# Column hats made on ScalarE from one loaded row of columns, in place of twelve hats loaded by DMA; two buffers of them instead of three

## What is computed

```python
x = x + _L0_conv_ref(_gn(x), ...)   # 3x3 convolution in Winograd form (6x6 tiles, weights given in the tile domain)
x = x + _L1_conv_ref(_gn(x), ...)   # offsets by a 3x3 convolution, then a deformable 3x3 convolution, 8 groups
x = x + _L2_conv_ref(_gn(x), ...)   # four 3x3 convolutions with one-bit weights, quantised activations
x = x + _L3_conv_ref(_gn(x), ...)   # 3x3 convolution, vertical edges, channel attention
return x
```

```python
y0 = jnp.floor(py)
x0 = jnp.floor(px)
corners = [(y0, x0, (y0 + 1 - py) * (x0 + 1 - px)), (y0, x0 + 1, (y0 + 1 - py) * (px - x0)),
           (y0 + 1, x0, (py - y0) * (x0 + 1 - px)), (y0 + 1, x0 + 1, (py - y0) * (px - x0))]
```

## Time and profile before

| | |
|---|---|
| median of 3 runs | 4374.5 us (4368.3 to 4380.27) |
| the profiled execution | 4387.05 us, its span 4385.2 us |
| busy, share of the span | TensorE 95%, GpSimd 70%, VectorE 67%, ScalarE 42% |
| granted TensorE clock, mean | 0.983 of full speed |
| DMA | 1022.94 MB, mean 233 GB/s |
| DMA queues, share of 16 engines | q1 474.56 MB, 35.8%; q10 342.81 MB, 23.7%; q0 201.52 MB, 16.1% |

### The profile page before, as it was taken

One profiled execution on the slowest core, in us unless ns is written; L12 is line 12 of the kernel. 1 busy time (PEld: TensorE's weight loads), 2 busy tenths in 40 slices (PEclk: granted clock), 3 DMA queues, 4 the chain that ended last, 5 costly groups with the idle time before them and its releaser, 6 DMA issues.

```text
span 4385.2 us, 67257 instructions
## 1 busy us (share of the span) xinstructions
PE 4187.6 (95%) x24997; PEld 2015.3 (46%) x24997; DVE 2945.6 (67%) x6076; ACT 1831.5 (42%) x2008; POOL 3077.7 (70%) x3094
## 2 busy tenths in 40 slices
PE   2899999999999999999999999999999999999993
PEld 2444444444444544444454444444444454444441
DVE  5656677667766766777677767766776676666553
ACT  1343444444444434444444444444444443444431
POOL 1777777777776767767777776777767677776740
PEclk8999999999999999999999999999999999999996
DMA  4677787878877787887878878787787878778762
GB/s 109 217 245 230 234 263 224 259 229 247 257 239 232 237 248 247 244 251 230 249 240 250 260 233 255 224 259 228 242 258 231 249 237 251 247 243 251 224 194 63
DMA packets 480252, 1022.94 MB, mean 233 GB/s; under 512 B 262164, under 2 KB 298356, under 8 KB 475636
## 3 DMA queue, kind: packets, MB, share of 16 engines
q1 hardware_dynamic: 311668, 474.56, 35.8%
q10 hardware_dynamic: 69984, 342.81, 23.7%
q0 software_dynamic: 98304, 201.52, 16.1%
HBM read 862.19 MB, written 73.20 MB: 213 GB/s over the span
## 4 chain that ended last, share of the span: by engine, by line
PE 81%; POOL 5%; DMA 5%; DVE 5%; issue 2%; SPq 2%; ACTq 1%; ACT 0%; POOLq 0%; DVEq 0%
PE ps_r L1489 58%; PE ps_y L1501 6%; PE ps_c L1475 6%; POOL ring L600 5%; PE ps_a L1428 3%; DMA taps_c<-plane_act 3%; PE ps_c L1515 2%; PE ps_a L1475 1%; PE ps_y L1522 1%; PE ps_a L1466 1%; DMA plane_act<-act_c 1%; PE ps_c L1570 1%; DVE work_c L1271 1%; PE ps_c L1548 1%; ACTq L790 1%
## 5 line engine op out<-in xcount | busy, mean ns | idle before, releaser
L600 POOL DMA_INDIRECT ring<-patch_table,idx_part x3072 | 3069.5, 999 | 1153.9 <-issue 1001.5
L1489 PE MATMUL ps_r<-select,image 128*128 128x512 f32 x6912 | 3151.4, 601 | 14.1 <-DVE col_hat L1195 9.5
L1489 PEld LDWEIGHTS ps_r<-select,image 128*128 128x128 f32 x6912 | 1259.6, 191 | 1401.6 <-issue 1383.6
L1195 DVE TENSOR_TENSOR col_hat<-ps_r,col_hat 128x512 f32<-128x512 f32 x1152 | 793.0, 688 | 1219.4 <-PE ps_r L1489 1215.1
L650 ACT ACTIVATE select<-row_in,minus_row 128x1536 f32<-128x1536 f32 x384 | 604.6, 1575 | 994.4 <-PE ps_r L1489 615.9
L652 ACT ACTIVATE select<-select,one_col 128x1536 f32<-128x1536 f32 x384 | 605.4, 1577 | 12.5
L669 ACT COPY samples<-ps_c 128x512 f32<-128x512 f32 x256 | 148.8, 581 | 638.3 <-PE ps_c L1515 638.1
L1501 PEld LDWEIGHTS ps_y<-col_hat,w_dense 128*32 128x32 f32 x9216 | 228.2, 109 | 291.1 <-issue 289.5
L1501 PE MATMUL ps_y<-col_hat,w_dense 128*32 128x128 f32 x9216 | 331.2, 277 | 0.0
L1204 DVE TENSOR_TENSOR ps_w<-ring,ps_w 128x384 f32<-128x384 f32 x512 | 284.5, 556 | 40.2 <-DMA ring<-patch_table,idx_part 35.9
L1210 DVE TENSOR_TENSOR ring<-ring,ps_w 128x384 f32<-128x384 f32 x512 | 279.9, 547 | 4.4
(11 more groups left out here) (231 smaller groups left out, 2414.6 us busy)
## 6 DMA issues: line engine op xcount, KB each, us to landing
row_in<-coord_table ACTq DMA_DIRECT2D x384, 768.0 KB
col_hat<-coord_table SPq DMA_DIRECT2D x384, 768.0 KB
ring<-patch_table,idx_part POOLq DMA_INDIRECT x3072
taps_c<-plane_act SPq DMA_DIRECT2D x135, 268.1 KB
coord_table<-wino SPq DMA_DIRECT2D x64, 216.0 KB
taps_c<-xn_c ACTq DMA_DIRECT2D x96, 130.0 KB
taps_c<-xn_c SPq DMA_DIRECT2D x96, 130.0 KB
plane_act<-act_c SPq DMA_DIRECT2D x180, 65.0 KB
```

The lines of the kernel that those rows point to most:

```text
L600: nc.gpsimd.indirect_dma_start(out=ring[j][:, h % 2, k, :], out_offset=None, in_=table, in_offset=bass.IndirectOffsetOnAxis(ap=idx_part[:, ...
L1195: v.tensor_tensor(hat_t, ps_r[:, (s + t) % 2], hat_t, ALU.mult).then_inc(tile_weighed, 1)
L1489: ins = mm(ps_r[:, (s + t) % 2], image[:, m, t], select[s % 2][:, m], start=(m == 0), stop=(m == PAIRS - 1))
```

## The change

The coordinates table now holds 7 rows for each part in place of 18: six for the row hats and the column coordinate itself. VectorE writes the column with one copy in place of 12 subtractions, and ScalarE's two activations in slot 21 are gone; SyncE waits for VectorE alone. For each slot SyncE loads 512 columns, broadcast over 128 partitions (256 KB written in place of 768 KB), into one of two `col_in` buffers. ScalarE makes the hats for slot s+1 in slot s (`make_cols`): three Abs activations of 128 x 512, each with its own column number as bias (`minus_col`), and one Relu of 128 x 1536 over all three. It waits for the DMA and for the fold that frees one of now two `col_hat` buffers. VectorE's `weigh_tile` waits for `cols_made` in place of the DMA. `load_cols` waits for `col_in_read`, which ScalarE raises behind `make_cols` two slots earlier, and no longer for `dense_folded`. The biases are made once at the start, by one GpSimd iota and eight small VectorE instructions.

```diff
@@ -56,7 +56,8 @@
 WT = WIN // WQ
-ROWS = 2 * PAIRS + WIN
+ROWS = 2 * PAIRS + 1
 EPS = 1e-5
...
@@ -229,7 +232,8 @@
         select = [sb(f"select{b}", [P, PAIRS, HALF]) for b in range(2)]
-        col_hat = [sb(f"col_hat{b}", [P, WT, HALF]) for b in range(3)]
+        col_in = [sb(f"col_in{b}", [P, HALF]) for b in range(2)]
+        col_hat = [sb(f"col_hat{b}", [P, WT, HALF]) for b in range(2)]
         image = sb("image", [P, PAIRS, WT, P])
...
@@ -453,13 +461,11 @@
                 part = coord_table[bass.ds((n % 2) * ITEMS + (dense_tap(e) * PARTS + g), 1), 2 * PAIRS * HALF:]
-                if not known_zero(n) or s >= 3:
-                    sp.wait_ge(dense_folded, (n * SLOTS + s - 2) * WT)
+                if not known_zero(n) or s >= 2:
+                    sp.wait_ge(col_in_read, n * SLOTS + s - 1)
                 if s == 0:
                     sp.wait_ge(coords_out, n * COORDS_OUT + COORDS_OUT)
-                sp.dma_start(col_hat[s % 3][:].rearrange("p t x -> p (t x)"),
-                             part.rearrange("o (w x) -> o w x", w=WQ).to_broadcast([C, WQ, WT * HALF])
-                             ).then_inc(col_hat_in[s % 3], 16)
+                sp.dma_start(col_in[s % 2][:], part.to_broadcast([P, HALF])).then_inc(col_in_in[s % 2], 16)
             def load_image(n):
...
@@ -504,7 +510,7 @@
                 if s == 21:
-                    sp.wait_ge(a_act.sem, a_act.at(n, "hats"))
+                    sp.wait_ge(a_dve.sem, a_dve.at(n, "columns"))
                     to = coord_table[bass.ds((n % 2) * ITEMS, ITEMS), :].rearrange("i (r j p) -> j i r p", r=ROWS, j=JB)
...
@@ -579,6 +585,8 @@
                                       allow_small_or_imprecise_dtypes=True))
+            chain.step(nc.gpsimd.iota(minus_part[:], pattern=[[0, 1]], base=0, channel_multiplier=-1,
+                                      allow_small_or_imprecise_dtypes=True))
             chain.step(nc.gpsimd.memset(one_col[:], 1.0))
...
@@ -650,6 +659,20 @@
                 nc.scalar.activation(sel, sel, ACT.Relu, bias=one_col[:], scale=-1.0).then_inc(select_made, 1)
+            def make_cols(n, s):
+                u = n * SLOTS + s
+                act.wait_ge(col_in_in[s % 2], (n * (SLOTS // 2) + s // 2 + 1) * 16)
+                if not known_zero(n) or s >= 2:
+                    act.wait_ge(dense_folded, (u - 1) * WT)
+                hats = col_hat[s % 2]
+                for t in range(WT):
+                    nc.scalar.activation(hats[:, t], col_in[s % 2][:], ACT.Abs, bias=minus_col[:, t:t + 1]
+                                         ).then_inc(tiles_far, 1)
+                act.wait_ge(tiles_far, (u + 1) * WT)
+                nc.scalar.activation(hats[:], hats[:], ACT.Relu, bias=one_col[:], scale=-1.0).then_inc(cols_made, 1)
+                act.sem_inc(col_in_read, 1)
             def place_image(n, ts):
...
@@ -732,12 +755,6 @@
                     place(n, 1)
-                if s == 21:
-                    act.wait_ge(a_dve.sem, a_dve.at(n, "columns"))
-                    cols = coords_t[:, 2 * PAIRS:]
-                    chain.step(nc.scalar.activation(cols, cols, ACT.Abs))
-                    nc.scalar.activation(cols, cols, ACT.Relu, bias=one_col[0:DSEL], scale=-1.0).then_inc(a_act.sem, 1)
             def c_early(n, s):
...
@@ -827,6 +844,8 @@
                     place_image(n + 1, (0, 1))
+                if live(n + (s + 1) // SLOTS):
+                    make_cols(n + (s + 1) // SLOTS, (s + 1) % SLOTS)
                 if e == DT - 1 and live(n):
...
@@ -1146,15 +1165,7 @@
                     chain.join()
-                    for w in range(WIN):
-                        ins = v.tensor_scalar(coords_t[:, 2 * PAIRS + WT * (w % WQ) + w // WQ], turned_in[:, 1], float(w),
-                                              None, ALU.subtract)
-                        if w == WIN - 2:
-                            chain.add(ins)
-                            chain.join()
-                        elif w < WIN - 1:
-                            chain.add(ins)
-                    ins.then_inc(a_dve.sem, 1)
+                    v.tensor_copy(coords_t[:, 2 * PAIRS], turned_in[:, 1]).then_inc(a_dve.sem, 1)
                 lo = hat[:, 0].rearrange("p d q k -> p (d q k)")
...
@@ -1189,9 +1200,9 @@
                 if t == 0:
-                    dve.wait_ge(col_hat_in[s % 3], (n * (SLOTS // 3) + s // 3 + 1) * 16)
+                    dve.wait_ge(cols_made, n * SLOTS + s + 1)
                 dve.wait_ge(rows_made, tile + 1)
-                hat_t = col_hat[s % 3][:, t]
+                hat_t = col_hat[s % 2][:, t]
                 v.tensor_tensor(hat_t, ps_r[:, (s + t) % 2], hat_t, ALU.mult).then_inc(tile_weighed, 1)
...
@@ -1383,6 +1394,14 @@
             chain.step(v.tensor_scalar(minus_row[:], minus_row[:], ROUND, ROUND, ALU.add, ALU.subtract))
+            chain.step(v.tensor_scalar(minus_col[:, 0:1], minus_part[:], 1.0 / WQ, 0.5 - 0.5 / WQ, ALU.mult, ALU.add))
+            chain.step(v.tensor_scalar(minus_col[:, 0:1], minus_col[:, 0:1], ROUND, ROUND, ALU.add, ALU.subtract))
+            chain.step(stt(minus_col[:, 0:1], minus_col[:, 0:1], -float(WQ), minus_part[:], ALU.mult, ALU.add))
+            for t in range(1, WT):
+                chain.add(v.tensor_scalar(minus_col[:, t:t + 1], minus_col[:, 0:1], -float(WQ * t), None, ALU.add))
+            chain.join()
+            v.memset(hidden[:], 0.0).then_inc(columns_known, 1)
             dve.wait_ge(zeroed, 4)
```

More of the change, by code:

```diff
@@ L81 @@
 A_ACT = ([f"freq{a}" for a in range(FREQ)] + ["conv", "std1", "offconva", "offconvb"]
-         + [f"patch{j}" for j in range(NPATCH)] + ["coords", "hats"])
+         + [f"patch{j}" for j in range(NPATCH)] + ["coords"])
 C_DVE = ["moments2", "spread2", "norm2", "relu0", "down", "relu1", "relu2", "x3", "moments3", "spread3", "norm3", "edges",
@@ L192, in build @@
         minus_row = sb("minus_row", [P, 1])
+        minus_part = sb("minus_part", [P, 1])
+        minus_col = sb("minus_col", [P, WT])
         group_mask = sb("group_mask", [P, 8])
@@ L293, in build @@
         coords_out = sem("coords_out")
+        columns_known = sem("columns_known")
+        col_in_read = sem("col_in_read")
+        tiles_far = sem("tiles_far")
+        cols_made = sem("cols_made")
         row_in_in = [sem(f"row_in_in{b}") for b in range(2)]
-        col_hat_in = [sem(f"col_hat_in{b}") for b in range(3)]
+        col_in_in = [sem(f"col_in_in{b}") for b in range(2)]
         gathered = [sem(f"gathered{j}") for j in range(RING)]
@@ L328, in build @@
         sel_next = t_flat[:, 3 * P:3 * P + 3 * DSEL].rearrange("p (d s) -> p d s", d=3)
-        assert ROWS * P == FREQ * TR * FREQ * TC and 3 * (P + DSEL) <= 4 * Q * TAPS
-        coords_t = v_flat.rearrange("p (r s) -> p r s", s=P)[0:DSEL]
+        assert 3 * (P + DSEL) <= 4 * Q * TAPS
+        coords_t = v_flat[0:DSEL, 0:ROWS * P].rearrange("p (r s) -> p r s", s=P)
         image_next = t_flat[:, 0:PAIRS * WIN * C]
@@ L614, in _ @@
             act.wait_ge(idents_ready, 2)
+            act.wait_ge(columns_known, 1)
             act.wait_ge(vec_in, 16 * (2 * STRIPS + 1))
@@ L1502, in fold_dense @@
                                  w_dense[:, DT - 1 - e].rearrange("p g o -> p (g o)"),
-                                 col_hat[s % 3][:, t, j * P:(j + 1) * P], start=(e == 0 and t == 0), stop=False)
+                                 col_hat[s % 2][:, t, j * P:(j + 1) * P], start=(e == 0 and t == 0), stop=False)
                     ins.then_inc(dense_folded, 1)
```

## The result

The changed kernel takes 4396.0 us, the median of 6 runs (4392.8 to 4406.5); the kernel before 4379.5 in the same rounds (4368.3 to 4382.7). The ratio is 1.0046, 95% interval 1.0031 to 1.006: slower by 0.46%. In a second series, of 11 runs, it was 1.0029 (1.0018 to 1.004). The forecast was 4372 us, no difference; the time lies inside the wide range (4350 to 4408), outside the forecast's own (4361 to 4384), and on the wrong side. The profiled execution took 4395.2 us.

A forecast was written before the change was run, and what follows sets the result against it. The prediction took TensorE's matmuls to bound the kernel. From 4375 us it took 7 for taps waits and 5 for the first item, added 9 for ScalarE's new waits: 4372 us, range 4350 to 4408, the forecast's own 4361 to 4384.

The forecast's parts named there:

- The bound: Inside the loop an item lasts as long as its matmuls: TensorE busy 259.6 of 260 us.
- the single events: TensorE waits with lower clock near 1325 (7.2 us) and 4088 (4.8), together 12.0, taken as absent from a median run.
- The price of `make_cols`: ScalarE's three Abs at 0.62 and Relu at 1.58: 3.45 us per slot, bounds 3.3 to 3.9; ScalarE about 3107 us.
- ScalarE's new waits, +9: Slots 12 to 14, 3 to 6 and 23 to 1: together 0.6 us in each of 15 items, bounds 0 and about 50.
- The lighter DMA, -7: SyncE's smaller column load shortens TensorE's waits for taps_c: two thirds of 10.4 us, bounds 0 and -10.4.
- my base without the single event: TensorE's taps_c waits inside the loop: 14.2 less 3.7, 10.4 us left.
- the signs that I named: New profile: ScalarE about 3100 us, taps_c waits under 5, samples and select waits under 1 per item, DMA share well below 0.80.
- The first item, -5: Up to 418 us, weigh_tile waits behind gathers, 12.7 us with lower clock, shrink by 5, bounds 0 and -12.7.
- The smaller loads relieve nothing: All loads: if DMA time goes by number of pieces, nothing lands sooner and new waits remain: 4392 us, chance 0.13.
- ScalarE late by microseconds: Slot 6's row load lands no sooner, so samples in slot 5 and slots 12 to 14 wait: 4404 us, chance 0.23.
- Everything goes: All TensorE waits for taps (-10.4) and in the first item (-12.7) vanish without new ones: 4352 us, chance 0.22.
- My base of 4375: Whole execution: profiled 4387.05 us less 12.0 for two waits assumed absent from a median run.

The follow-up runs named there:

- the heavy loads kept: The kernel before plus five Abs of 128 x 448 per slot on ScalarE where the changed kernel has make_cols, DMA loads unchanged: ratio 1.0229.
- the light load alone: The changed kernel without the work of make_cols (ScalarE only signals by an Abs of 128 x 1, hats are zeros): ratio 0.9989 to the kernel before.
- one issue moved: The changed kernel with SyncE's load of the next image x moved from slot 10 to slot 11, behind the taps load: ratio 0.9958 to the kernel before.
- a second profile: Profile of the kernel before with only SyncE's x load moved from slot 10 to slot 11: ratio 0.9978.
- the second profile: Profile of the changed kernel run again without an edit: ratio 1.0029 to the kernel before, items 3762.9 us.
- moving one or the other: The changed kernel with either slot 11's row load issued in slot 10 (0.9971) or the x load moved to slot 11 (0.9958), against the kernel before.

## Why the prediction was wrong, point by point

**The bound: right.** An item is its matmuls; with no wait it takes 259.8 us. At most 24 us were to be had from the items (3752.5 against 3728.4), the single events among them.

**The price of `make_cols`: right.** Three Abs in 1.93 us (1.86 forecast) and a Relu of 1.576: 3.5 us against 3.45; ScalarE 3083 us against 3107.

**ScalarE's new waits, +9: too high.** 2.0 us, all in slot 0; none in slots 14 and 5, which I priced at 0.4 and 0.15 in each item. For slot 14 two thirds of the 7.99 us row are 5.3, so TensorE starts its tile at 2094.5 to 2094.6 and not at 2094.4: the room was 0.2 us or more, not 0.1. With the heavy loads kept, about the same occupation brings 12.5 us for samples, so the light load seems to help there too.

**The lighter DMA, -7: the step that failed.** Its mechanism holds: with the light load alone the waits for the taps go nearly all, from 13.6 to 1.1 us, and in the changed kernel those in slots 14 and 15 are gone. But I took the rest of the DMA's schedule as fixed. The sentence "In a plain slot nothing is: ScalarE spends 3.2 us on `select` and 3.45 on the hats" asks which instruction of ScalarE is late for TensorE. What stood behind `make_cols` in every slot is the next row load, a DMA issue. I followed it only in slots 3 to 6, as a delay of `select`. In slot 11 it falls into the stretch of another engine's load, 4.3 us later than before, and the waits there grew from 9.2 to 22.6 us. All waits for the taps are 22.6 us against 10.4 in my base without the single event: +12.2 in place of -7. My range for it, 0 to -10.4, left out a loss, though nothing excluded one. Of the signs that I named, this is the one that failed: under 5 us of waits for the taps.

**The first item, -5: not there.** The row tiles start at 119.8 instead of 123.0, 3.2 us sooner, against a forecast of 0. The waits for `weigh_tile` are 11.9 us (9.5 before): GpSimd is as busy as before from 100 to 640 us (411 us in both), and I read it so that TensorE, sooner there, waits for the same gathers; no run tests this.

**The rivals.** The time came nearest to "The smaller loads relieve nothing" (4392), by luck: the light load alone relieves 12.5 us of waits. "ScalarE late by microseconds" (4404) is 8 us off and has the sign, but works by another way: its mark, the wait for `samples` in slot 5, is absent. "Everything goes" (4352) holds with the light load alone for the taps, and its price was too high: the first item's waits for `weigh_tile` stay (14.9 us there). The changed kernel reaches 0.9958 with one issue moved.

**The sum.** My base of 4375 took the two events out of every run; the kernel before has a median of 4379.5 in six runs, and a second profile has both events, so that the base was some us too low is likely. Against it the items took 3753.8 in place of 3752.5 - 12.0 = 3740.5 us, +13.3, of which the waits in slot 11 are 19.7 - 9.8 = 9.9 and the fold 2.0; the rest, 1.4, is not assigned. Up to the first `hidden`: +7.0, which makes 4395.3; that this is the time of the execution follows from how the parts are cut and proves nothing. In the second profile the two parts are +22.4 and +3.1: its items hold more waits of over 2 us, and behind one of them, 2.7 us long, the clock is 0.83 over 20 us (1030 to 1050), which is 3.4 us more. The 7 us of the first profile are for the most part slot 11 again. The first item waits there 2.9 us in place of 0.6, with a clock of 0.83 behind (500 to 520 us above), and in the kernel before that stretch has the full clock:

```profile
500.00:520.00 20.00, 19.38 (x110) 9.05 (x107) 12.89 (x27) 6.28 (x9) 15.43 (x16) 1.00 0.88 253
```

That is 2.3 + 20 x 0.17 = 5.7 us. In the second profile the wait is 2.0 us and the clock 0.91, so 1.4 + 1.8 = 3.2 us, where 3.1 are missing.

## What to carry to other kernels

Work added to an engine delays the DMAs that this engine issues behind it, and a large load that slips by 4 us can cost more through another queue's transfer than the work costs by itself. So for each issue that moves, list what is issued on all queues from a few us before it to the next deadline, with sizes, and ask which transfer there is waited for last. When a transfer has a deadline, order what need not be there behind it. Move one issue at a time: moving one or the other brought 0.6 to 0.7% here, moving all row loads made new collisions.

## What the runs showed of the hardware

One load of 768 KB, issued 4.5 us later in each item with no other edit, cost 1.47%. While its 768 KB passed, SyncE's queue moved 0.16 MB in 3 us where it had moved 0.79. The mean DMA share told nothing of this: the changed kernel waits longer for the taps at 0.69 than the kernel before at 0.80, and even in the 40 us around slot 11, nearly full in both, its share is the lower one. Before (as above, TensorE alone):

```profile
2324.00:2364.00 40.00, 39.58 (x251) 1.00 0.98 278
```

After:

```profile
2334.00:2374.00 40.00, 38.83 (x242) 1.00 0.91 248
```
